# Direct weight splitting on GpSimd, and the first projection unit ahead of the last value product

## The reference

```python
# layer 0: 16 heads of 16, one shared key and value head, causal; then a router over 64 experts
x = x + ga * attn0(norm(x));  x = x + gb * route0(norm(x))
# layer 1 attention: 16 heads of 128, causal, rms-normed q and k
q, k, v = (x @ Wq.T), (x @ Wk.T), (x @ Wv.T)
q, k = rmsnorm(q, gq), rmsnorm(k, gk)
attn = softmax(mask(q @ k.T * hd ** -0.5)); out = (attn @ v) @ Wo.T
# layer 1 feed-forward: each weight is lut[idx], a table of 16 values looked up by an int32 index
gate = x @ lut[gate_idx].T; up = x @ lut[up_idx].T          # 688 x 256 each
y = (silu(gate) * up) @ lut[down_idx].T                     # 256 x 688
```

## Time and profile before

| | |
|---|---|
| median of 3 runs | 1359.11 us |
| the three runs | 1359.11, 1360.73, 1351.29 us |
| the profiled execution's own time | 1358.34 us |
| its span, first to last instruction | 1356.5 us |
| mean granted TensorE clock | 0.949 |
| busy: PE, DVE, ACT, POOL | 89%, 68%, 51%, 53% |

### The profile page before, as it was taken

The page is one execution under the profiler, slowest core; times in us unless marked ns, Lnnn a source line. Parts: engine busy times, 40 slices in busy tenths (PEclk is TensorE's granted clock), DMA queues, the critical chain, the costliest instruction groups (busy, mean ns, idle before and its releaser), DMA issues.

```text
span 1356.5 us, 22769 instructions
## 1 busy us (share of the span) xinstructions
PE 1207.7 (89%) x6940; PEld 878.5 (65%) x6940; DVE 923.2 (68%) x2757; ACT 685.7 (51%) x1599; POOL 719.5 (53%) x773
## 2 busy tenths in 40 slices
PE   6879897988579999999999999999999999964998
PEld 5435454545457677677777676776776776753787
DVE  5757677774566686786776866866777867852553
ACT  3345545564364654645645546546546546451442
POOL 0344101111124698889457898875588888862000
PEclk8788889998779999999999999999999999996999
DMA  6433312100033200220330310113420110011000
GB/s 222 129 124 121 125 48 69 42 33 1 32 134 119 64 31 32 112 73 1 112 118 29 134 63 11 42 60 104 132 104 23 35 39 8 6 36 34 16 17 31
DMA packets 39956, 90.39 MB, mean 67 GB/s; under 512 B 9529, under 2 KB 23713, under 8 KB 38865
## 3 DMA queue, kind: packets, MB, share of 16 engines
q1 hardware_dynamic: 27312, 51.32, 11.2%
q0 software_dynamic: 11424, 34.08, 7.7%
q10 hardware_dynamic: 1152, 4.19, 0.8%
HBM read 61.00 MB, written 28.43 MB: 66 GB/s over the span
## 4 chain that ended last, share of the span: by engine, by line
PE 49%; DVE 13%; issue 7%; ACT 3%; DVEq 0%; ACTq 0%
PE bank L1474 10%; PE bank L298 8%; PE bank L299 8%; PE bank L300 8%; PE bank L1453 8%; PE bank L1464 4%; DVE qk L1078 3%; PE bank L1440 3%; DVE qkst L1054 2%; DVE negmax L1149 2%; ACT pT L866 1%; DVE probs L1144 1%; DVE x L1134 1%; PE bank L1454 1%; DVE ytmps L1131 1%
## 5 line engine op out<-in xcount | busy, mean ns | idle before, releaser
L677 POOL TENSOR_SCALAR gtmp<-gidx,lut 128x344 f32<-128x344 int32 (+2 forms) x210 | 294.1, 1400 | 21.3
L680 POOL TENSOR_TENSOR gacc<-gacc,gtmp 128x344 f32<-128x344 f32 (+2 forms) x210 | 181.4, 864 | 17.5
L1453 PE MATMUL bank<-kT,qT 128*128 128x128 f32 (+3 forms) x512 | 180.7, 443 | 9.3 <-ACT probs L874 9.3
L1474 PE MATMUL bank<-pT,v 128*128 128x512 f32 (+3 forms) x512 | 150.9, 438 | 12.2 <-ACT pT L866 12.1
L874 ACT ACTIVATE probs<-bank,negmax 128x128 f32<-128x128 f32 (+3 forms) x256 | 135.3, 529 | 51.4 <-DVE negmax L1149 47.8
L1149 DVE TENSOR_REDUCE negmax<-bank 128x1 f32<-128x128 f32 (+3 forms) x256 | 123.3, 484 | 47.9 <-PE bank L1454 46.2
L1054 DVE BATCH_NORM_STATS2 qkst<-qk 128x6 f32<-128x128 f32 x512 | 110.5, 279 | 64.3 <-issue 64.3
L298 PE MATMUL bank<-wgH,hL 128*128 128x512 f32 x384 | 153.7, 400 | 0.0
L1088 DVE TENSOR_REDUCE negmax<-bank 128x1 f32<-128x512 f32 (+3 forms) x176 | 108.3, 636 | 65.5 <-PE bank L1383 64.9
L299 PE MATMUL bank<-wgL,hH 128*128 128x512 f32 x384 | 152.2, 396 | 0.0
L300 PE MATMUL bank<-wgH,hH 128*128 128x512 f32 x384 | 151.9, 396 | 0.0
(11 more groups left out here) (219 smaller groups left out, 2772.7 us busy)
## 6 DMA issues: line engine op xcount, KB each, us to landing
hH<-h_saved SPq DMA_DIRECT2D x16, 512.0 KB, 4.1
hL<-h_saved SPq DMA_DIRECT2D x16, 512.0 KB, 4.9
qst<-q_parts SPq DMA_DIRECT2D x96, 64.0 KB, 2.4
sraw<-in_wqkv POOLq DMA_DIRECT2D x32, 192.0 KB, 3.1
w_saved<-shi POOLq DMA_DIRECT2D x32, 192.0 KB, 2.2
w_saved<-slo POOLq DMA_DIRECT2D x32, 192.0 KB, 2.4
wgH<-w_saved SPq DMA_DIRECT2D x4, 1536.0 KB, 7.5
wgL<-w_saved SPq DMA_DIRECT2D x4, 1536.0 KB, 10.8
```

The costliest lines, as they stand in the source:

```text
L677: link(pool.tensor_scalar(tmp if j else acc, part, float(j), lut1[0:rows, j:j + 1], ALU.is_equal, ALU.mult))
L680: link(pool.tensor_tensor(acc, acc, tmp, ALU.add))
L1453: pe.matmul(bank[SCORE_BANKS[i % 3]][:, 0:n], qT[:, h, t * P:n], kT[:, h, 0:n], start=True, stop=False)
L1474: last = pe.matmul(bank[7][:, k * P:], v1[:, k, h * HD1:(h + 1) * HD1], pT1[:, h % 2, at:at + (QT - k) * P], start=(k == 0), stop=(k == QT ...
```

## The change

1. Group 0's q, k and v weights are no longer stored to DRAM: POOL splits eight parts straight into `wgH` and `wgL` during layer 0, with two buffers for the raw part so that the next part's load is in flight. Its output-projection weights are split straight into `woH` and `woL` (`split_wo0`, two parts of 512 columns) after layer 0.
2. Groups 1 to 3 still go through DRAM, in eight parts of 512 columns each where twelve were, with the next part's load issued before the split of this one. The wait for the stores of the part before now stands ahead of that load.
3. The table lookup loads its indices one job ahead and splits each result straight into the feed-forward tiles. The stores to `wffn_saved` and the six strips are gone. PE's wait is now for 14 jobs.
4. SP no longer loads group 0's weights (two transfers in layer 0, two at the start of layer 1).
5. PE computes unit 0 of the next round's projections inside the attention, ahead of the last value product; ACT copies it out ahead of the last `oH1`. The round then starts with unit 1, and the wait for the exponentials stands before unit 2 (the first that uses a score bank). The wait for the next group's weights moves into the attention with it.
6. So that these waits are right for every round, PE's rounds are written out as eight copies of the round's code beside the first attention, five of them inside loops.

```diff
-WCH = 384
+WCH0 = 384
+WCH1 = 512
...
-        sraw1 = sb(s1, "sraw1", [P, WCH])
+        sraw1 = sb(s1, "sraw1", [P, 2, WCH1])
...
-        gidx = sb(s1, "gidx", [P, PIECE], I32)
+        gidx = sb(s1, "gidx", [P, 2, PIECE], I32)
...
             def load_w1(g):
-                sp.wait_ge(w1_stored, (g + 1) * len(W_PARTS) * 32)
+                sp.wait_ge(w1_stored, g * PARTS1 * 32)
...
-                if b == 1:
-                    load_w1(0)
...
-            sp.wait_ge(h1_stored, NB * 32)
-            load_wo(0)
...
+            def load_part(i):
+                src, raw = part_of[i]
+                to = raw[:, i % 2, :]
...
+                if i >= 2:
+                    pool.wait_ge(part_lo, i - 1)
+                pool.dma_start(to, src).then_inc(part_loaded[i % 2], 16)
+
+            def split_part(i, hi, lo, more):
+                raw = part_of[i][1][:, i % 2, :]
+                if more:
+                    load_part(i + 1)
+                pool.wait_ge(part_loaded[i % 2], (i // 2 + 1) * 16)
+                pool.tensor_copy(hi, raw).then_inc(part_hi, 1)
+                pool.wait_ge(part_hi, i + 1)
+                pool.tensor_tensor(lo, raw, f32(hi), ALU.subtract).then_inc(part_lo, 1)
...
+            load_part(0)
+            for i in range(PARTS0):
+                cols = slice(i * WCH0, (i + 1) * WCH0)
+                split_part(i, wgH_cols[:, cols], wgL_cols[:, cols], i + 1 < PARTS0)
...
+            def split_w1(g):
+                first = PARTS0 + PARTS_WO + (g - 1) * PARTS1
+                load_part(first)
+                for c in range(PARTS1):
+                    if g > 1 or c:
+                        pool.wait_ge(w1_stored, ((g - 1) * PARTS1 + c) * 32)
+                    split_part(first + c, shi1[:, :], slo1[:, :], c + 1 < PARTS1)
+                    pool.wait_ge(part_lo, first + c + 1)
+                    for k, part in enumerate((shi1, slo1)):
+                        pool.dma_start(w1_saved[g - 1, k, :, c * WCH1:(c + 1) * WCH1], f32(part[:, :])).then_inc(w1_stored, 16)
...
+            split_wo0()
+            load_job(0)
...
-                pool.dma_start(part, src).then_inc(loaded_idx, 16)
-                pool.wait_ge(loaded_idx, (i + 2) * 16)
-                if i:
-                    pool.wait_ge(gat_dma, i * 16)
+                if i + 1 < len(jobs):
+                    load_job(i + 1)
+                pool.wait_ge(loaded_idx[i % 2], (i // 2 + 1) * 16)
+                pool.wait_ge(f_lo, i)
...
-                pool.dma_start(wffn_saved[:, to:to + cols], gacc[:, 0:cols]).then_inc(gat_dma, 16)
...
-                pool.dma_start(wraw[:, 0:cols], wffn_saved[:, frm:frm + cols]).then_inc(f_loaded, 16)
-                pool.wait_ge(f_loaded, (i + 1) * 16)
-                pool.tensor_copy(hi, raw).then_inc(f_hi, 1)
+                pool.tensor_copy(hi, gacc[:, 0:cols]).then_inc(f_hi, 1)
                 pool.wait_ge(f_hi, i + 1)
-                pool.tensor_tensor(lo, raw, f32(hi), ALU.subtract).then_inc(f_lo, 1)
+                pool.tensor_tensor(lo, gacc[:, 0:cols], f32(hi), ALU.subtract).then_inc(f_lo, 1)
...
                     i = s - LAG1 - 2
+                    if i == ITEMS - 1 and not last:
+                        copy1(it + 1, 0)
...
                     i = s - LAG1 - 1
+                    if i == ITEMS - 1 and weights is not None:
+                        pe.wait_ge(*weights)
+                        pe.wait_ge(h1_loaded, (it + 2) * 32)
+                        pe.wait_ge(tr_act, (it + 1) * 2 * QT)
+                        project1(it + 1, 0)
...
-                pe.wait_ge(h1_loaded, (it + 1) * 32)
-                pe.wait_ge(exp1, it * ITEMS)
-                for u in range(3 * QT):
-                    if u < 3:
-                        pe.wait_ge(tr_act, it * 2 * QT)
+                for u in range(1, 3 * QT):
+                    if u == 2:
+                        pe.wait_ge(exp1, it * ITEMS)
                     project1(it, u)
...
-            pe.wait_ge(f_lo, 2 * KT + 2)
+            pe.wait_ge(f_lo, 2 * 2 * KT + MT)
```

More of the change, by code:

```diff
@@ L82 @@
 EARLY_NORM = 53
-WCH = 384
+WCH0 = 384
+WCH1 = 512
 WQKV = 3 * KT * HG * HD1
-W_PARTS = tuple((o, WCH) for o in range(0, WQKV, WCH)) + tuple((WQKV + h * D, D) for h in range(HG))
 WALL = WQKV + HG * D
+PARTS0 = WQKV // WCH0
+PARTS_WO = HG * D // WCH1
+PARTS1 = WALL // WCH1
 VW = 32
@@ new lines, in _, with split_wo0 @@
+            woH_cols, woL_cols = (w[:, :, :].rearrange("p h n -> p (h n)") for w in (woH, woL))
+            load_part(0)
+            for i in range(PARTS0):
+                cols = slice(i * WCH0, (i + 1) * WCH0)
+                split_part(i, wgH_cols[:, cols], wgL_cols[:, cols], i + 1 < PARTS0)
+            def split_wo0():
+                load_part(PARTS0)
+                for c in range(PARTS_WO):
+                    cols = slice(c * WCH1, (c + 1) * WCH1)
+                    split_part(PARTS0 + c, woH_cols[:, cols], woL_cols[:, cols], c + 1 < PARTS_WO)
@@ L663, in _, with load_job @@
+            jobs = [(a[f"idx_{w}"][k * P:(k + 1) * P, o:o + PIECE], P, PIECE, wguH[:, i, k, o:o + PIECE], wguL[:, i, k, o:o + PIECE])
+                    for i, w in enumerate(("gate", "up")) for k in range(KT) for o in range(0, INTER, PIECE)]
+            jobs += [(a["idx_down"][m * P:min((m + 1) * P, INTER), :], min(P, INTER - m * P), D, wdH[:, m, :], wdL[:, m, :])
                      for m in range(MT)]
+            def load_job(i):
+                src, rows, cols, hi, lo = jobs[i]
+                pool.dma_start(gidx[0:rows, i % 2, 0:cols], src).then_inc(loaded_idx[i % 2], 16)
@@ new lines, in _ @@
+            load_job(0)
+            pool.memset(f32(wguH[:, :, :, INTER:]), 0.0).then_inc(f_zero, 1)
+            pool.memset(f32(wguL[:, :, :, INTER:]), 0.0).then_inc(f_zero, 1)
+            pool.wait_ge(loaded_lut, 16)
+            for i, (src, rows, cols, hi, lo) in enumerate(jobs):
+                if i in (0, 4, 8):
+                    split_w1(1 + i // 4)
+                part, acc, tmp = gidx[0:rows, i % 2, 0:cols], gacc[0:rows, 0:cols], gtmp[0:rows, 0:cols]
+                if i + 1 < len(jobs):
+                    load_job(i + 1)
+                pool.wait_ge(loaded_idx[i % 2], (i // 2 + 1) * 16)
+                pool.wait_ge(f_lo, i)
@@ L850, in _, with attend1 @@
             act.wait_ge(gqk_ready, 18)
-            def attend1(it, norm=False):
+            def attend1(it, last=False):
                 for u in range(2 * QT):
@@ L875, in attend1 @@
                                        bias=negmax[:, i:i + 1], accum_out=sums[:, i:i + 1]).then_inc(exp1, 1)
-                    if norm and s == NORM_PARTS:
+                    if last and s == NORM_PARTS:
                         norm_f1.act_scale(act, 0, 1)
                     i = s - LAG1 - 2
+                    if i == ITEMS - 1 and not last:
+                        copy1(it + 1, 0)
                     if i >= 0 and i % QT == QT - 1:
@@ L1442, in turn1, with attend1 @@
                     last.then_inc(tr_pe, 1)
-            def attend1(it):
+            def attend1(it, weights=None):
                 for s in range(ITEMS + LAG1 + 1):
```

117 lines of the change are left out of this document (45 added, 72 removed).

## The result

| | before | after |
|---|---|---|
| median, first measurement | 1355.97 us (4 runs) | 1313.37 us (4 runs, 1310.77 to 1316.33) |
| ratio, with its 95% interval | | 0.9686 [0.9641, 0.9732] |
| profiled execution, span | 1358.34, 1356.5 us | 1310.77, 1309.0 us |
| mean granted TensorE clock | 0.949 | 0.971 |

Measured twice more, the changed kernel gave 1311.67 us, 0.9711 [0.9674, 0.9748], and 1312.45 us, 0.9705 [0.9672, 0.9737]. The gain is 40 to 43 us by medians and 47.5 us between the two profiled executions.

The account below looks back on a forecast made before the run. Layer 1 was taken as PE's, with one 28.3 us hole from POOL's chain; 1356.5 - 30.6 - 11.3 + 0 - 2 - 2 = 1310.6 us of span, hence 1313 us measured, range 1303 to 1328.

Parts of the forecast that it names:

- Part 1, the hole: PE's wait ahead of the feed-forward closes as POOL ends near 1122 us: 28.3 us, plus 2.3 us of cold start.
- Part 2, unit 0: Unit 0 ahead of the value product covers PE's 0.76 us wait in 15 rounds: -11.3 us, ends 0 and -15.
- The rival that ACT's order gives it back: DVE's chain to the next attention starts as late as before, so PE waits 0.76 us again: 1324 us, chance 0.12.
- Part 3, copies of the round: Round joins in PE's longer program cost 0; bounds -1 and +3 us for the outer loop's return over three copies.
- Part 4, POOL beside DVE: Layer-1 rounds beside lookups and splits: POOL's shifted work and idle end give -2 us, bounds -6 and +5.
- the prediction's own signs of being wrong: Rounds not shorter though the hole is gone, DVE's busy time per round up, or a gap before unit 1.
- POOL's density costs rounds: Lookups and splits fall worse, and each of 11 rounds beside them costs 1.2 us more: 1326 us, chance 0.12.
- Part 5, layer 0: POOL's stores and SP's reload of group 0 leave the queues in layer 0: -2 us, bounds 0 and -8.
- The waits that I had pointed at: In layer 0, PE waits 9.4 us in four pieces for the maxima's transfers between 62 and 137 us.

Follow-up runs that it names:

- e8: The kernel before, unaltered, measured and profiled again: 1350.79 us, ratio 0.9984.
- e4: The changed kernel, unaltered, measured and profiled again: 1311.67 us.
- e3: The kernel before with only the lookups' part of POOL's change (indices a job ahead, results split straight into the feed-forward tiles, no strips): 1323.32 us, ratio 0.9797.
- e6: The kernel before with only the attention-weight part of POOL's change (group 0 direct, 512-column parts, loads one ahead): 1324.15 us, ratio 0.9791.
- e2: The changed kernel with PE's and ACT's order of before (unit 0 behind the value product), POOL's changes kept: 1325.66 us, ratio to the kernel before 0.9809.
- e1: The kernel before with only unit 0 moved ahead of the last value product, POOL untouched: 1349.40 us, ratio 0.9985.
- e5: The changed kernel with 15 of 16 comparisons and all 15 additions left out of each lookup job: 1294.36 us, ratio to the kernel before 0.9567.
- e7: The changed kernel with POOL pausing in seven rounds until DVE has done its norm chain and first multiplication: 1300.78 us, ratio to the kernel before 0.9614.
- e10: Control on the changed kernel: eight POOL pauses in the middle of each attention, not during the norm chain: 1313.93 us, ratio to the kernel before 0.9715.
- e11: The changed kernel with group 0's q, k and v parts stored to DRAM and read back in layer 0: 1316.61 us, ratio to the kernel before 0.9743.
- e12: The changed kernel, unaltered, measured once more as a base on the same chip: 1312.45 us.

## Why the prediction came true, and where it was wrong

**Part 1, the hole** (-30.6). The mechanism held: 28.3 us gone, the feed-forward 1.8 us shorter where 2.3 was worked out. In the pair of e8 and e4 the two are 31.5 and 1.0 us, so the exact 28.3 belongs to the execution that it was read from. POOL ended 6 us before the 1122 predicted; but it had also started its layer-1 chain 11.8 us earlier, at 376.26, so the chain was 740 us long where 734 was worked out. A split's period was 6.2 us (6.1 predicted), a group 384.70 to 438.48, 53.8 us (50): eight periods do not hold because in one the stores took longer, the wait of 5.77 us in the row above, for stores issued just behind two loads of 512 KB each that SP had issued from 421.37 on (that these are the cause is argued, from the order alone); the median of such a store is 2.6 us from issue to landing. `split_wo0` took 7.3 us (10), and a job's join 2.2 us (2.4). None of these errors could matter, since POOL ended 79 us ahead of PE, and the prediction had counted on at least 70. e3 and e6 add what it did not see: half of the work would have been enough.

**Part 2, unit 0** (-11.3). The mechanism is as described, in the waits and in the join's timeline. Its size was a little low: 14.0 us between e2 and e4, close to the upper of the two ends given. The shortest round is 51.4 us in the kernel before (51.3 in e8) and 50.3 in e1, which is 1.0 to 1.1 us less where the wait alone is 0.76; what more lies in the 14.0 is not taken apart. The rival that ACT's order gives it back is refuted by e2 against e4. What the prediction missed is that this part needs part 1 to be worth anything (e1), and not only for the hole: without it unit 0 meets the group's weights in flight.

**Part 3, copies of the round** (0, up to +3). The join of two rounds costs nothing in any other place, and the outer loop's one return over three copies does cost something, once:

```profile
771.75 0.47 PE L297 MATMUL bank<-wgH,hL 128*128 128x512 f32 x1 [1.11 <-issue]
```

1.1 us, 0.8 to 1.2 in the other runs with this code, within the bound. It is where the rule of the Trainium skill ("Runtime: NRT & Kernel Launch", instruction fetch mechanics) would put a stall; the trace gives its size and that the shorter loops inside have none. That the fetch is its cause no run here shows.

**Part 4, POOL beside DVE** (-2, from -6 to +5). This is the step that failed, in its sign. I priced the lookups by the extremes of the rounds of before, counted on the last round being freed (it was, by 1.0 us: 39.74 to 38.74 from its transposes on), and took splitting's greater density as a bound rather than as the likely case. e2 and e6 measured it: the attention is 5 to 9 us longer with the dense splits (842.7 and 842.8, against 834.0 and 837.3), at or beyond the bound of +5, and e3 shows that the lookups' side adds nothing that the two profiles of before can tell. Of the prediction's own signs of being wrong, one came true: DVE's busy time rose, from 923.2 to 935.0 us on the page. And PE's wait for the scores, 13.1 us in the changed kernel, had been shorter:

```profile
PE bank L1453 <- ACT probs L874: 9.3, 7, 2.1
```

It was the rival "POOL's density costs rounds", to which I gave 0.12, at about half its size. That the total came out right all the same is in part luck: part 2 gave 2.7 us more, and the sum started from a high execution (part 5). e5 gives the whole price of the lookups beside DVE, 21 us in the profile and 17 by medians, and e7 where 11 of them are paid: in the norm chain ahead of each attention. By windows of three rounds of the changed kernel, as in the earlier trace rows:

```profile
479.20:531.70 52.50, 50.51 (x275) 38.02 (x273) 40.21 (x122) 28.41 (x72) 48.97 (x43) 1.00 0.11 35
636.40:687.00 50.60, 50.24 (x275) 38.01 (x274) 38.98 (x120) 28.60 (x72) 34.62 (x38) 1.00 0.30 103
950.90:1002.70 51.80, 50.29 (x274) 37.94 (x273) 39.40 (x123) 28.58 (x72) 47.58 (x48) 1.00 0.19 74
```

PE is busy 50.2 to 50.5 us in each; what a round takes beyond it follows POOL's busy time only loosely, since it depends on where POOL's work falls in the round (e10). Why splits, which have pauses of their own, cost the attention 5 us or more, and whether it is their density or where they came to stand, was not separated. The norm chain is not where: its mean is 5.51 and 5.46 us in e2 and e6, and 5.43 and 5.49 before and in e8.

The rule quoted from the Trainium skill ("GPSIMD Engine Reference", key points) had the right sign here, against my sum: among the DVE instructions that contend with POOL it names those with two SBUF inputs, and the multiplications, 700 ns in e5 and 832 here, are of these. It also names a 2-port mode; whether the normalising instruction, which has one tensor input, runs in one, no run here shows. On POOL's side e5 took out comparisons and additions together and can't say which of them is to blame, but the trace of the changed kernel can. Of the small operations of the norm chains, 60 ran with no arithmetic of POOL's beside them: their median is 0.19 us, the longest 0.22. Beside comparisons alone, 137 ran: median 0.19, longest 0.50. Beside two-input operations alone (additions and subtractions), 45 ran: median 0.62, longest 1.33. It is mostly the additions that stretch the chain.

**Part 5, layer 0** (-2, from 0 to -8). The -11.8 of the first pair is mostly that one execution of before; about half of it is a stretch in which PE ran below its upper level. The ends of layer 0 in the profiles are 378.25, 369.84, 372.39 and 368.33 in the four whose layer 0 is that of before (before, e8, e1, e3), and 365.4 to 371.4, with a mean of 368.3, in nine others that split group 0 directly. Without the first the difference is 2 us, with it 4; but two of the three others lie among the nine and the third is 1 us above them, so the profiles do not show a saving in layer 0 for certain. The waits that I had pointed at did not shrink either: PE's wait for the maxima between 62 and 137 us is 9.9 us in six pieces in the changed kernel, where the earlier trace rows has 9.4. e11 puts the saving at 4.2 us by medians, inside the bounds, and its profile has it in the attention. So the size agrees, and where I placed it is not borne out. The sum was also made against an execution that was 6 us slower than the median of 17 later runs, and a part of the agreement is luck: the predicted 1313 was built on a start which later measurements put at 1351 to 1353. From there the same terms would have given 1306, and e4 and e12 gave 1312. The missing 6 us are of the size of part 4's error, less what part 2 gave more.

## What to carry to other kernels

Find out which engine has slack after a change and spend it on not disturbing the one that sets the pace: POOL had 79 us to give, and seven waits beside DVE's norm chain bought 11 us more, while eight elsewhere bought none. A part of a change can be worth nothing by itself (e1), and two parts can each bring the same 28 us that they bring together only once (e3, e6), so measure each alone; these runs tell more of this change than its total does. And before a stage's difference between two profiles is explained, look at the granted clock of identical work in both and profile each kernel once more.

## What the runs showed of the hardware that I had not expected

- **Small DVE operations suffer most from POOL.** A 128x32 operation takes 0.19 us alone and 0.62 (median) beside POOL's two-input operations, and hardly more than alone beside its comparisons; the large ones of 128x512 take 16% less without the lookups. In the chain of 17 dependent ones shown above this is 1.7 us (3.90 to 5.61), on the path, and 1.6 to 1.8 us in the mean of all rounds. POOL pays too: its comparison took 2.25 us in the row above, beside DVE's multiplications, where 1.44 is usual. DVE's maxima, which read PSUM, take the same beside either (483 ns in the changed kernel, 486 in e5).
- **The granted clock falls in one execution and not in another, for the same instructions.** It fell in the same place in three of the profiles (before, e1, e12), and while PE's rows show it busy: in the kernel before, these are two windows of 5 us inside the stretch shown above, and PE was at work in all of both.

```profile
185.00:190.00 5.00, 5.00 (x33) 3.81 (x33) 4.79 (x14) 1.48 (x4) 0.00 (x0) 0.72 0.00 0
190.00:195.00 5.00, 5.00 (x25) 2.24 (x23) 4.22 (x9) 1.88 (x4) 0.00 (x0) 0.59 0.02 2
```

  A clock of 0.5 would be the lower level, 1.2 GHz, for the whole window, and 0.59 is most of one at that level. What sets off these falls no run here shows.
- **A loop's return over three copies of a round costs PE 0.8 to 1.2 us**, a return over one round nothing, nor one over two copies in the kernel before, whose only wait without a releaser is the 28.3 us.
